# Adding expert outputs into the result by accumulating scatters

## What is computed

```
x  = x + gnn(xn) + mix(xn)
t  = layernorm(x)
rw, re = top_k(softmax(t @ router.T), 2);  rw = rw / rw.sum()
out = t
for e in range(8):
    out = out + combine[:, e] * (gelu(t @ w1[e] + b1[e]) @ w2[e] + b2[e])
x  = x + out
```

## Time and profile before

| | us |
|---|---|
| median of three runs | 1010.29 |
| lowest, highest | 1008.53, 1013.03 |
| span of the profiled execution | 1013.6 |
| busy in it: PE / DVE / ACT / POOL | 859.1 / 644.0 / 416.8 / 699.5 |

### The profile page before, as it was taken

The page is one execution under the profiler, slowest core; times in us unless marked ns, Lnnn a source line. Parts: engine busy times, 40 slices in busy tenths (PEclk is TensorE's granted clock), DMA queues, the critical chain, the costliest instruction groups (busy, mean ns, idle before and its releaser), DMA issues.

```text
span 1013.6 us, 19598 instructions
## 1 busy us (share of the span) xinstructions
PE 859.1 (85%) x6332; PEld 528.8 (52%) x6332; DVE 644.0 (64%) x2171; ACT 416.8 (41%) x1087; POOL 699.5 (69%) x503
## 2 busy tenths in 40 slices
PE   3878878988999999999999999999399961999930
PEld 2433433435445444545545555555398851899920
DVE  3699998896576365365455665656667764555534
ACT  3544543332454334334334443443144441666620
POOL 4788888888887878888778888887403568544420
PEclk7699998996999999999999999999699975999975
DMA  9865664545465555455546565435944424344459
GB/s 292 172 112 85 97 119 57 83 60 104 70 132 90 81 89 81 73 103 81 91 52 104 79 129 76 49 35 77 295 130 116 126 85 136 109 132 126 128 135 271
DMA packets 144169, 113.10 MB, mean 112 GB/s; under 512 B 106847, under 2 KB 129955, under 8 KB 143942
## 3 DMA queue, kind: packets, MB, share of 16 engines
q1 hardware_dynamic: 79988, 71.74, 25.3%
q0 software_dynamic: 56928, 25.42, 24.0%
q10 hardware_dynamic: 7154, 14.68, 4.6%
HBM read 72.00 MB, written 40.89 MB: 111 GB/s over the span
## 4 chain that ended last, share of the span: by engine, by line
PE 37%; POOL 10%; DMA 7%; DVE 5%; issue 4%; ACT 1%; ACTq 0%; SPq 0%; POOLq 0%; DVEq 0%
POOL edge_sums L694 9%; PE ps L1321 5%; PE ps L1532 5%; PE ps L1543 5%; PE ps L1461 3%; PE ps L1128 3%; DMA edge_sums<-sums,addr 3%; DMA r2t<-expert_outputs 2%; PE ps L1271 2%; PE ps L1257 2%; PE ps L1308 2%; PE ps L1517 1%; PE ps L1451 1%; PE ps L1297 1%; POOL routed_rows L713 1%
## 5 line engine op out<-in xcount | busy, mean ns | idle before, releaser
L694 POOL DMA_INDIRECT edge_sums<-sums,addr x360 | 565.7, 1571 | 136.7 <-issue 105.0
L1684 DVE TENSOR_SCALAR oh<-node,dsrc 128x500 bf16<-128x500 int16 (+1 forms) x392 | 116.7, 359 | 73.3 <-PE ps L1321 73.0
L921 ACT ACTIVATE r<-ps 128x500 f32<-128x500 f32 (+1 forms) x224 | 103.4, 549 | 72.0 <-PE ps L1257 71.9
L1321 PE MATMUL ps<-oh,r2t 128*64 128x500 bf16 (+1 forms) x1176 | 130.7, 359 | 1.4 <-DVE oh L1684 1.4
L1128 PE MATMUL ps<-edges,same 128*128 128x65 f32 x720 | 101.2, 286 | 12.1 <-ACT sums L754 4.6
L1647 DVE TENSOR_TENSOR r2t<-ps,r 125x4096 f32<-125x4096 f32 x25 | 110.3, 4413 | 0.0
L1128 PEld LDWEIGHTS ps<-edges,same 128*128 128x128 f32 x720 | 91.8, 200 | 35.5 <-issue 28.2
L1587 DVE SCALAR_TENSOR_TENSOR same<-srow,src_f,below 128x128 f32<-128x128 int32 x360 | 103.6, 345 | 3.6 <-DMA srow<-in_src_row 2.7
L1321 PEld LDWEIGHTS ps<-oh,r2t 128*64 128x64 bf16 x1176 | 59.1, 110 | 71.2 <-issue 39.2
L725 POOL DMA_INDIRECT expert_outputs<-r x56 | 54.4, 972 | 56.0 <-DVE r L2043 51.2
L1175 PE MATMUL ps<-r2t,r 125*32 125x512 f32 x400 | 60.1, 727 | 34.2 <-DVE r2t L1647 34.2
(11 more groups left out here) (284 smaller groups left out, 1381.7 us busy)
## 6 DMA issues: line engine op xcount, KB each, us to landing
srow<-in_src_row SPq DMA_DIRECT2D x45, 512.0 KB
edges<-in_edge_attr SPq DMA_DIRECT2D x22, 512.0 KB
r<-routed_rows SPq DMA_DIRECT2D x56, 129.0 KB, 2.1
r<-hpre_rows SPq DMA_DIRECT2D x12, 500.0 KB, 4.2
edge_sums<-sums,addr POOLq DMA_INDIRECT x360
r2t<-in_ew SPq DMA_DIRECT2D x4, 1024.0 KB, 9.3
hpre_rows<-r ACTq DMA_DIRECT2D x16, 250.0 KB, 2.5
edge_sums<-r SPq DMA_DIRECT2D x4, 884.0 KB, 13.9
```

The costliest lines, as they stand in the source:

```text
L694: pool.indirect_dma_start(out=tables[k], out_offset=bass.IndirectOffsetOnAxis(ap=addr[:, j:j + 1], axis=0), in_=sums[:, j % OR, :], in_off ...
L921: act.activation(phT[:, R % 2, h, 0:n], bank(BP[h], 128, 0, n), ACT.Square).then_inc(pair_squares, 1)
L1321: m = mm(ps[EA * a:EA * (a + 1), BD * BANK:BD * BANK + n], lhsT=parts3[:, (DCH - 1 - 2 * w // DW) * DW + (2 * w + a) % DW, s, :], rhs=oh[: ...
L1684: v.tensor_scalar(oh[:, (2 * i + a) % OHS, 0:nt * P].rearrange("p (t n) -> p t n", t=nt), node16[:, 0:nt, :], dsrc[:, 2 * w + a:2 * w + a ...
```

## The change

The result's DRAM tensor gets 128 spare rows behind its N rows. Each piece of `x_res` is finished (residual plus token term) between the routing batches on POOL, in six pieces (`KEPT`) instead of five, and SP stores it to the result: three pieces before it waits for the routing table, three after it has issued the loads of steps 0 to 3. The expert steps then add their weighted rows straight into the result. The indices of both experts are the node's own row; pad rows go to the spare rows, which POOL fills with zeros early on. There is no table `expert_outputs`, no read-back, no final add and no final store.

Two adds into the same row must not be in flight together. Rows of one expert are all different; rows of two experts may meet. So DVE makes a further table, `turn_i`: for the first step of an expert and for an empty step it holds the count of `ys_stored` at which the step just before has landed, for others a count reached long ago. POOL reads a step's entry with a `value_load`, waits on that register, and in every step also waits for the landing of the step two before. The first scatter waits for all the stores of the result's base.

```diff
+    KEPT = ((0, 4), (4, 8), (8, 12), (12, 17), (17, 22), (22, T))
+    BASE = 16
+    SPARE = (0, 22, 44, 66, 88, 110, 128)
...
-        youts = nc.dram_tensor("expert_outputs", (2 * N, C), fp32, kind="Internal").ap()
...
+            def keep_rows(g):
+                sp.wait_ge(residual, g + 1)
+                t0, t1 = KEPT[g]
+                for a, z in PARTS:
+                    sp.dma_start(out[0:N, :].rearrange("(p t) c -> p t c", p=P)[a:z, t0:t1, :], x_res[a:z, t0:t1, :]
+                                 ).then_inc(rows_kept, 16)
+            for g in range(3):
+                keep_rows(g)
...
                 for s, h, nth in filter(some, sts):
+                    if s == 4:
+                        for g in range(3, len(KEPT)):
+                            keep_rows(g)
                     row = sp.value_load(row_i[0:1, bass.ds(s, 1)], min_val=0, max_val=E * REG)
...
-                sp.wait_ge(ys_stored[h], 16 * ((NS - h + SB - 1) // SB))
...
-            for g in range(T // FT):
-                for a, z in PARTS:
-                    sp.dma_start(outputs_of(g)[a:z, 0, :, :], youts[0:N, :]
...
+                sp.wait_ge(ys_stored[h], BASE + 16 * ((NS - h + SB - 1) // SB))
...
-            pool.iota(pad_rows[:, C + 1:XF], [[0, 1]], base=2 * N, channel_multiplier=1,
+            pool.iota(pad_rows[:, C + 1:XF], [[0, 1]], base=N, channel_multiplier=1,
...
+            for k in range(SB):
+                pool.dma_start(out[N + SPARE[k]:N + SPARE[k + 1], :], pad_rows[SPARE[k]:SPARE[k + 1], 0:C]).then_inc(ys_stored[k], 16)
             pool.wait_ge(mean_ready, 1)
...
-            for g in range(T // FT):
-                xv = x_res[:, g * FT:(g + 1) * FT, :]
-                pool.tensor_tensor(xv, xv, xl_all[0:P, g * FT:(g + 1) * FT, 0:C], ALU.add).then_inc(residual, 1)
+                for g in ((0,), (1, 2), (), (), (3, 4, 5))[b]:
+                    k0, k1 = KEPT[g]
+                    xv = x_res[:, k0:k1, :]
+                    pool.tensor_tensor(xv, xv, xl_all[0:P, k0:k1, 0:C], ALU.add).then_inc(residual, 1)
+
+            pool.wait_ge(table_ready, 3)
 
             def scatter_outputs(sts):
                 for s, h, nth in filter(some, sts):
+                    turn = pool.value_load(turn_i[0:1, bass.ds(s, 1)], min_val=BASE, max_val=BASE + 16 * NS) if s else None
                     pool.wait_ge(ys_ready, s + 1)
                     pool.wait_ge(idx_ready, s + 1)
-                    pool.indirect_dma_start(out=youts, out_offset=bass.IndirectOffsetOnAxis(ap=y_idx[:, h:h + 1], axis=0),
-                                            in_=ys[:, h, :], in_offset=None, bounds_check=2 * N - 1, oob_is_err=False).then_inc(ys_stored[h], 16)
+                    if s == 0:
+                        pool.wait_ge(rows_kept, 32 * len(KEPT))
+                        for k in range(SB):
+                            pool.wait_ge(ys_stored[k], BASE)
+                    else:
+                        pool.wait_ge(ys_stored[(s - 1) % SB], turn)
+                    if s > 1:
+                        pool.wait_ge(ys_stored[(s - 2) % SB], BASE + 16 * ((s - 2) // SB + 1))
+                    pool.indirect_dma_start(out=out, out_offset=bass.IndirectOffsetOnAxis(ap=y_idx[:, h:h + 1], axis=0),
+                                            in_=ys[:, h, :], in_offset=None, compute_op=ALU.add).then_inc(ys_stored[h], 16)
...
-                v.tensor_scalar(twin[:, :, C + 1], dst_row[:, t0:t1], float(N), None, ALU.add)
+                v.tensor_copy(twin[:, :, C + 1], dst_row[:, t0:t1])
...
             link(v.tensor_reduce(row_f, pasts, AX.X, ALU.add))
+            link(v.scalar_tensor_tensor(turn_first, exp_f, float(E), step_row[:, :], ALU.is_ge, ALU.mult))
+            link(v.tensor_tensor(turn_first, row_f, turn_first, ALU.max))
+            link(v.tensor_tensor(turn_first, turn_first, step_row[:, :], ALU.is_ge))
...
             v.tensor_copy(exp_i[:, :], exp_f[0:1, :]).then_inc(table_ready, 1)
+            v.wait_ge(consts, 24)
+            v.scalar_tensor_tensor(turn_i[:, 1:NS], turn_first[0:1, 1:NS], 16.0, turn_at[0:1, 0:NS - 1], ALU.mult, ALU.add).then_inc(table_ready, 1)
...
-            for g in range(T // FT):
-                xv = x_res[:, g * FT:(g + 1) * FT, :]
-                v.wait_ge(node_rows[g], 32 + 64)
-                link(v.tensor_tensor(xv, xv, outputs_of(g)[:, 0, :, :], ALU.add))
-                v.tensor_tensor(xv, xv, outputs_of(g)[:, 1, :, :], ALU.add).then_inc(yb_added, 1)
```

More of the change, by code:

```diff
@@ L127, in gps_layer @@
         row_i = sb("row_i", [1, NS], i32)
+        turn_i = sb("turn_i", [1, NS], i32)
+        turn_at = sb("turn_at", [1, 66])
         rank8 = sb("rank8", [P, E])
@@ L267, in gps_layer @@
         y_w = carve([128, SB])
-        FT = 5
+        turn_first = carve([128, NS])
         b2_rows = srow[:, :, :].rearrange("p h c -> p (h c)").bitcast(fp32)[:, 0:E * C]
@@ L406, in gps_layer @@
         residual = sem("residual")
+        rows_kept = sem("rows_kept")
         table_ready = sem("table_ready")
@@ L420, in gps_layer @@
         ys_stored = [sem(f"ys_stored{h}") for h in range(SB)]
-        yb_added = sem("yb_added")
-        stored = sem("stored")
         program = ctx.enter_context(nc.Block())
@@ L485, in pair_of @@
             return t0 + 2 * k, min(t0 + 2 * k + 2, t1)
[L487 to L491, removed]
         def step_at(st, d):
@@ L627, in _ @@
             for h in range(SB):
-                sp.wait_ge(ys_stored[h], 16 * ((NS - h + SB - 1) // SB))
-            sp.wait_ge(ey_ps, NS)
-            sp.wait_ge(residual, T // FT)
-            for g in range(T // FT):
-                for a, z in PARTS:
-                    sp.dma_start(outputs_of(g)[a:z, 0, :, :], youts[0:N, :]
[L635 to L641, removed]
+                sp.wait_ge(ys_stored[h], BASE + 16 * ((NS - h + SB - 1) // SB))
         @program.gpsimd
@@ L682, in _ @@
             pool.memset(kd[:, :, :, D:D + 1], 1.0).then_inc(consts, 1)
+            pool.iota(turn_at[:, :], [[16, 66 // SB], [0, SB]], base=BASE, channel_multiplier=0,
+                      allow_small_or_imprecise_dtypes=True).then_inc(consts, 1)
             for g in range(NGR):
@@ L2040, in output_rows @@
                 wait(v, xs_loaded[h], nth * 16 + 16)
-                wait(v, ys_stored[h], nth * 16)
+                wait(v, ys_stored[h], nth * 16 + (BASE if nth else 0))
                 v.tensor_copy(y_w[:, h:h + 1], xs[:, h, C:C + 1])
@@ L2064, in _ @@
             steps(v, expert_steps, SB, 2)
-            v.wait_ge(residual, T // FT)
-            for g in range(T // FT):
-                xv = x_res[:, g * FT:(g + 1) * FT, :]
-                v.wait_ge(node_rows[g], 32 + 64)
-                link(v.tensor_tensor(xv, xv, outputs_of(g)[:, 0, :, :], ALU.add))
-                v.tensor_tensor(xv, xv, outputs_of(g)[:, 1, :, :], ALU.add).then_inc(yb_added, 1)
 def kernel(**inputs):
@@ L2099 @@
         args.append(nc.dram_tensor(f"in_{name}", a.shape, _mybir.dt.from_np(a.dtype), kind="ExternalInput").ap())
-    args.append(nc.dram_tensor("out_x", f["x"].shape, _mybir.dt.float32, kind="ExternalOutput").ap())
+    args.append(nc.dram_tensor("out_x", (n + 128, f["x"].shape[1]), _mybir.dt.float32, kind="ExternalOutput").ap())
     gps_layer(nc, *args)
     r = _run(nc, [arrays], core_ids=[0])
-    return r.results[0]["out_x"]
+    return r.results[0]["out_x"][:n]
```

## The result

The changed kernel takes 1035.97 us (median of 4 runs, 1035.16 to 1038.21) against 1011.66 of the kernel before beside it: ratio 1.0224, 95% interval 1.0195 to 1.0253. It is slower: the interval lies clear of 1, though its lower end is just short of 2%. The forecast was 1001.5. The profiled executions span 1036.4 and 1013.6 us.

A forecast was written before the change was run, and what follows sets the result against it. Transfers bound the last 37 us, TensorE the expert stage before. 866.8 + 2.3 + 45 x 2.03 + 10 x 4.06 + 3.76 = 1004.8 us against 1013.6, so median 1001.5; range 985 to 1026.

The forecast's parts named there:

- 0.30 is what POOL needs between two: Expert scatters on POOL: 0.30 us between two, taken from the edge sums, added to the landing time in each step's price.
- the forecast's own formula: Expert stage: an ordinary step costs the larger of 1.97 and (T + 0.30)/2 us, each of ten waiting steps T + 0.30.
- The step that built it: Landing of 1 KB adds: 3.26 us for a small add, plus 0.50 for 96 KB more as two plain passes: 3.76.
- The rival with T = 4.6: Longer landing, adds costing by the byte or meeting loads: steps 2.45 and 4.90 us, median 1029.7; chance 0.20.
- T: Time from the start of an adding expert scatter to its landing: 3.76 us taken, upper end 4.92.
- the prediction's own sign, steps of 2.4 or more: Expert scatters 2.4 us or more apart would show the longer landing; 2.03 apart would show the forecast right.
- The upper end of the range, 1026: Slow end of the forecast range for the whole kernel, 1026 us, taken at T = 4.5.
- The break-even "T = 4.02": Landing time of an adding scatter, 4.02 us, at which the change neither gains nor loses.
- the turn's read: POOL's read of a step's turn, 0.27 + 0.15 us, taken as hidden; rival read in line: median 1012.3, chance 0.13.
- The span ending at its landing: End of the program: no read-back after the last scatter, the span ending when that scatter lands, at 1004.8 us.
- the 870 that the prediction named as a sign of being wrong: First expert scatter: forecast at 866.8 + 2.3 us; a start later than 870 would make the prediction wrong.
- read PSUM or are no copies: Routing stage: reason for counting no DVE hold-up from POOL's early residual adds, where 6.4 us at most was possible.

## Why the prediction was wrong

**The step that failed: "0.30 is what POOL needs between two".** The row shows two adds that follow each other without waiting for a landing. I charged it for the way from a landing to the next start. That way is 0.78 us in ordinary steps and 0.84 in waiting ones, since the wait stands in an instruction ahead of the scatter; moved onto the scatter, it is 0.27. By the forecast's own formula the ordinary step is (3.85 + 0.78) / 2 = 2.315 and the waiting one 3.85 + 0.84 = 4.69; 45 and 10 of them make 151.1 us in place of 132.0. That is 19.1 of the 24.8 us: 16.2 by the hand-over, the rest by a landing 0.09 longer. The other 5.7 us are in the ordinary steps, 2.44 us on the mean (the ten waiting ones come to 4.70). TensorE is not their cause: from the first turn of expert on, each scatter's outputs had been ready for 4 us or more when it started. One landing in ten takes over 4.25 us, which goes that way; whether it is all of it was not tried.

The trace of before does have landings that end a wait, in the edge sums. One of them, in the chain of that kernel:

```profile
587.96 7.79 DMA edge_sums<-sums,addr
595.75 0.27 issue
596.01 0.81 POOL edge_sums L694
```

The hand-over is 0.27 us there too, for that add carries its wait itself. So this row would have confirmed the 0.30. What the forecast left out is that the new waits stand in instructions of their own.

**Right: the landing.** 3.76 was taken, 3.85 measured (median; eight in ten lie from 3.75 to 4.25). The step that built it was right too: 0.60 + 0.50 = 1.10 us of engine time for an add, 1.15 measured. By the two source reads of the Trainium skill (Collectives: The Full Stack, The bandwidth ceiling), which that page counts for ReduceScatter, it would be an estimated 0.66; the trace has 1.15 and decides. The rival with T = 4.6 had 2.45 and 4.90 for the steps and 1029.7 in all, near what was seen, but for another reason: T was not longer, the way behind it was. By the prediction's own sign, steps of 2.4 or more, that rival would have been read out of the result; only T as measured rules it out. The upper end of the range, 1026, was worked out from T alone and stopped short of this rival's 1029.7. The break-even "T = 4.02" was one for T + 0.30 = 4.32, and the sum came to 4.63.

**Right: POOL's price, the turn's read, the mechanism.** Scatters of 1.55 us; ten long gaps where they were forecast (4.51 to 4.95 us for 4.06); the read of the turn hidden, since scatters with it follow each other at 1.85 us as the edge sums do without it; POOL waiting for its own transfers, and TensorE idle behind it.

**Missed: the end.** "The span ending at its landing" did not hold: POOL's last instruction outlasts the last landing by 5.2 us. It was in the trace of before, hidden by the tail that the change removes. Taking a tail away uncovers what lay beneath it, and I named no such row.

**Right in part: the moved parts.** The start is 870.52 for 869.1, beyond the 870 that the prediction named as a sign of being wrong. POOL's last piece ended at 861.2, not 858.4, and the stores of the result's base were down at 867.6, not 866. What the first scatter waited for last was its own outputs, which ACT finished at 869.76; ACT took the late step 4 first. TensorE's timeline:

```profile
868.50 0.44 PE L1514 MATMUL ps<-ident,r 128*128 128x128 f32 x2 [1.85 <-DMA r<-routed_rows]
```

The lateness of this load was foreseen, at 2.3 us behind 864.17; it is 4.3. The residual adds cost no time that the runs with them elsewhere would show, but not for the reason given, that the long DVE instructions there "read PSUM or are no copies": short ones were held up, by 6.2 us in all.

What the change as such is worth is seen with the waits cut to what the data need: 39.4 us from the last scatter's start to the end become 9.1, the expert stage gives 16.1 back (123.5 for 107.4), and the first scatter starts 1.2 earlier. That makes 15.4 us of the profiled spans (998.2 for 1013.6); the same kernel's other profiled execution spans 1006.7, 6.9 less. By the ratios it is about 1%.

## What to carry to other kernels

Price an ordering wait as landing plus hand-over, and read the hand-over from a place where a landing really ended the wait and the wait stands as the new one will, not from back-to-back work; then order a step's waits so that the instruction itself carries the one that ends last. Before making accumulating transfers wait for each other, ask which of them can meet in a row: here a wait in 7 of 55 steps was needed, and those of the other ordinary steps cost 21 us, those of the empty ones 8 to 12. When a change removes the end of a program, list what had been running beneath it.

## What the hardware showed that was not expected

- From a landing to the start of the scatter that waits for it, it takes 0.27 us when the scatter carries the wait and 0.78 to 0.93 when it stands in an instruction ahead (a semaphore instruction, or an addition of one element).
- POOL's last instruction of the program takes 9.07 to 11.2 us in the thirteen profiled executions, with plain scatters (10.66 and 10.75) as with adding ones, and ends 5 to 8 us after the last landing. In all eleven executions with adding scatters it ends 8.85 or 8.86 us after the last one's start, whether that lands in 2.7 us (an empty step that writes nothing) or in 3.8: it does not follow the landing. Why was not tried.
- POOL's adds of two arrays in SBUF held up VectorE's instructions of 0.2 us for almost their whole length, 2.03 and 4.53 us beside adds of 2.17 and 4.32.
- Adding transfers took 1.15 us of each DMA engine where plain ones took 0.33, and cost the stage some 3.8 us as long as nobody waited for them.
